# Preparation of a patch-attention kernel: one-pass prelu, weights loaded earlier, and unused matmuls in TensorE's pauses

## The reference, cut to what matters

```python
def prelu(x, a): return jnp.where(x >= 0, x, a * x)
x = gn(x)                                          # mean and variance per channel
embed_w  = prelu(conv1x1(x, Wa, ba), aa)           # 32 channels, 48 x 48
match_in = prelu(conv1x1(x, W1, b1), a1)           # 16 channels, 48 x 48
ref = prelu(conv1x1(pool2x2(x), W2, b2), a2)       # 16 channels, 24 x 24
w  = patches3x3(ref);  wn = w / max(norm(w), 1e-4) # 576 keys of 144
xp = patches3x3(match_in)                          # 2304 queries of 144
y  = softmax(10 * wn @ xp, over keys)              # 576 x 2304
# patches of embed_w, weighted by y, are overlapped and convolved with Wd (stride 2)
```

## Time and profile before

| | us |
|---|---|
| median of 3 runs (lowest, highest) | 326.76 (324.23, 326.82) |
| profiled execution | 326.36 |
| its span | 324.6 |
| PE busy | 259.4 (80%) |
| DVE busy | 173.8 (54%) |
| ACT busy | 133.1 (41%) |
| POOL busy | 98.6 (30%) |

### The profile page before, as it was taken

One profiled execution on the slowest core, in us unless ns is written; L12 is line 12 of the kernel. 1 busy time (PEld: TensorE's weight loads), 2 busy tenths in 40 slices (PEclk: granted clock), 3 DMA queues, 4 the chain that ended last, 5 costly groups with the idle time before them and its releaser, 6 DMA issues.

```text
span 324.6 us, 4740 instructions
## 1 busy us (share of the span) xinstructions
PE 259.4 (80%) x1698; PEld 240.2 (74%) x1698; DVE 173.8 (54%) x368; ACT 133.1 (41%) x269; POOL 98.6 (30%) x101
## 2 busy tenths in 40 slices
PE   0459529936396979997998999999998899998075
PEld 0448428926375859996998989999987799997074
DVE  3864623254746673377225745555696854543822
ACT  2060236254346452445335674547645442122020
POOL 2710122038546220523514051517845600000000
PEclk9999999577657575599759999999999999999655
DMA  3030034420003000134300000000120000000241
GB/s 73 0 48 3 9 67 72 104 70 2 1 0 50 2 1 0 14 61 72 56 3 0 2 0 3 0 2 0 38 37 2 0 3 0 2 0 2 44 65 36
DMA packets 11495, 7.67 MB, mean 24 GB/s; under 512 B 8497, under 2 KB 10609, under 8 KB 11345
## 3 DMA queue, kind: packets, MB, share of 16 engines
q1 hardware_dynamic: 11264, 7.09, 12.2%
q10 hardware_dynamic: 208, 0.30, 0.3%
HBM read 2.14 MB, written 1.18 MB: 10 GB/s over the span
## 4 chain that ended last, share of the span: by engine, by line
PE 51%; DVE 20%; issue 9%; SPq 9%; ACT 6%; POOL 2%; DMA 2%; DVEq 0%; ACTq 0%; POOLq 0%
PE zt L727 20%; PE yt L742 8%; PE ps L707 5%; PE pm L681 4%; SPq L377 3%; SPq L373 3%; PE pm L621 3%; DVE negm L1156 3%; PE pm L774 3%; PE pm L660 2%; DVE mimg L1078 2%; DVE yl L1171 2%; DVE bnst L988 2%; PE pd L754 2%; DVE mimg L1075 2%
## 5 line engine op out<-in xcount | busy, mean ns | idle before, releaser
L727 PE MATMUL zt<-ident,nt 128*125 128x128 f32 (+1 forms) x720 | 98.0, 290 | 0.0
L727 PEld LDWEIGHTS zt<-ident,nt 128*125 128x125 f32 (+1 forms) x720 | 94.0, 191 | 1.4 <-issue 0.3
L528 POOL TENSOR_TENSOR nt<-nt 128x599 f32<-128x599 f32 (+1 forms) x42 | 56.4, 1342 | 47.9 <-ACT nt L907 40.8
L1171 DVE TENSOR_TENSOR yl<-zt,yh 125x384 fp32r<-125x384 f32 (+1 forms) x60 | 33.4, 557 | 43.9 <-ACT yh L915 15.2
L915 ACT ACTIVATE yh<-zt 125x384 fp32r<-125x384 f32 (+1 forms) x60 | 29.2, 486 | 44.1 <-PE zt L727 44.1
L899 ACT ACTIVATE nt<-ps,negm 128x576 f32<-128x576 f32 x32 | 23.7, 742 | 56.5 <-DVE negm L1156 56.5
L707 PE MATMUL ps<-wh,mh 128*128 128x288 f32 x64 | 18.3, 372 | 17.0 <-POOL mr L522 12.3
L907 ACT ACTIVATE nt<-nt,rps 128x599 f32<-128x599 f32 x36 | 28.6, 795 | 7.1 <-DVE rps L1163 6.9
L1156 DVE TENSOR_REDUCE negm<-ps 128x1 f32<-128x576 f32 x32 | 24.1, 753 | 13.1 <-PE ps L707 13.0
L742 PE MATMUL yt<-yh,kh 125*128 125x384 f32 (+1 forms) x60 | 25.6, 427 | 4.6 <-DVE yl L1171 4.5
L1194 DVE SCALAR_TENSOR_TENSOR v<-pd,v 32x384 f32<-32x384 f32 (+3 forms) x48 | 26.3, 547 | 2.4 <-PE pd L754 0.9
...
## 6 DMA issues: line engine op xcount, KB each, us to landing
...
```

Source lines behind the costliest of these rows:

```text
L528: pool.tensor_tensor(nt[:, dst, (to + 1) * KP + 1:(to + 1) * KP + 1 + n], nt[:, one, (row1 + 1) * KP + 1:(row1 + 1) * KP + 1 + n], nt[:, o ...
L727: last = nc.tensor.matmul(turned(zt[:, m % 2, :], n, dh, col, JW), keys_at(tile, r + dr, n, shift), ident[:, :], start=at == 0, stop=at == ...
L1171: nc.vector.tensor_tensor(yl[0:n, blk, :].rearrange("p (h j) -> p h j", j=W), turned(zt[:, m % 2, :], n), F(yh[0:n, blk, :]).rearrange("p ...
```

## The change

1. **One-pass prelu.** The conv weights and biases of a convolution are multiplied by a sign (1 for slopes up to 1, else -1), so that prelu becomes the larger of `v + bias` and `slope * (v + bias)`. ACT writes `slanted = slope * v + slope * bias` (`slant`), DVE one pass, `max(v + bias, slanted)`, for each part. The signs are taken back in the keys' scale (`kscale`) and in the output weights (POOL, one product more). DVE computes the signs (`slope_signs`) before the statistics and waits there for the parameters.
2. **Match image.** The parts of `conv1` no longer write the copied rows; two DVE copies of 336 columns do, after the eighth part.
3. **Order of preparation.** `weights` is put before `low`; W2, W1, Wa are scaled and split one after another; `bias` becomes three jobs, of which the third (Wa) comes after `split`. The eight parts of `conv1` follow one another and `norm` comes behind them. In `SPREAD` the jobs of image 1 move likewise by up to two thirds of a step.
4. **Loads.** SP issues two quarters of `x`, then the output weights, all of image 1, the residual images and the cosine matrix, and only then the patches. ACT issues the other two quarters ahead of the parameters.
5. **POOL and DVE.** POOL zeroes `wdf` and the borders of `nt` at the start; `emb`, `mr`, `wr` are zeroed by DVE. POOL handles the output weights right after `mean` of image 0.
6. **Unused matmuls.** `idle(n)` issues n fp32 matmuls of 128 x 128 on `ones` into `yt`, which nothing reads: 14 before the mean, 5 before the first bias, 2 before `norm`, 6 before `inorm`, 6 and 10 before the scores.

```diff
 BEFORE = [
-    ("xs", (0,)), ("mean", (0,)), ("low", (0,)), ("weights", (0,)), ("bias", (0,)), ("conv2", (0, 1)),
-    ("conv1", (0, 1)), ("squares", (0,)), ("conv1", (2, 3, 4)), ("norm", (0,)), ("conv1", (5, 6, 7)),
-    ("inorm", (0, 1)), ("keys", (0,)), ("split", (0, 1))]
+    ("xs", (0,)), ("mean", (0,)), ("weights", (0,)), ("bias", (0, 1)), ("conv2", (0, 1)), ("low", (0,)),
+    ("conv1", (0, 1)), ("squares", (0,)), ("conv1", (2, 3, 4, 5, 6, 7)), ("norm", (0,)),
+    ("inorm", (0, 1)), ("keys", (0,)), ("split", (0, 1)), ("bias", (2,))]
+WARM = {("mean", 0): 14, ("bias", 0): 5, ("norm", 0): 2, ("inorm", 0): 6, ("keys", 0): 6, ("split", 0): 10}
...
-            load_x(0)
+            load_x(0, range(2))
+            output_weights()
+            load_x(1, range(4))
+            for b in range(B):
+                sp.dma_start(x1(b), x[b].rearrange("c h w -> c (h w)")).then_inc(s_xin[b], 16)
+            sp.dma_start(cosm[:, :], dct).then_inc(s_cos, 16)
             ref_patches(0)
             match_patches(0)
-            sp.dma_start(x1(0), x[0].rearrange("c h w -> c (h w)")).then_inc(s_xin[0], 16)
-            load_x(1)
-            output_weights()
-            sp.dma_start(cosm[:, :], dct).then_inc(s_cos, 16)
-            sp.dma_start(x1(1), x[1].rearrange("c h w -> c (h w)")).then_inc(s_xin[1], 16)
...
-            first = before.index(("low", 0, 0))
+            first = before.index(("squares", 0, 0))
+            zeros()
+            pool.wait_ge(s_tiles, NPOOL_EDGES)
             perform(before[:first], handlers)
-            zeros()
-            pool.wait_ge(s_tiles, NTILE_EDGES)
+            output_weights()
+            pool.wait_ge(s_wd, 1)
             perform(before[first:], handlers)
-            output_weights()
...
+            def idle(n):
+
+                for _ in range(n):
+                    nc.tensor.matmul(yt[:, 0:128], ones[:, :], ones[:, :], start=True, stop=True)
...
-            perform(before, handlers)
+            pe.wait_ge(s_const, 2)
+            for name, b, k in before:
+                idle(WARM.get((name, k), 0))
+                handlers.get(name, lambda b, k: None)(b, k)
             scores(0)
...
-                if k % 2:
-                    nc.scalar.activation(zneg[0:rows, 1, :], o[0:rows, 0:HALF], ACT.Relu,
-                                         bias=nbias[0:rows, which:which + 1], scale=-1.0)
-                nc.scalar.activation(z[0:rows, k % 2, :], o[0:rows, 0:HALF], ACT.Relu,
-                                     bias=bias[0:rows, which:which + 1]).then_inc(s_z, 1)
+                nc.scalar.activation(slanted[0:rows, k % 2, :], o[0:rows, 0:HALF], ACT.Identity,
+                                     bias=sbias[0:rows, which:which + 1],
+                                     scale=par[0:rows, P_A1 + which:P_A1 + which + 1]).then_inc(s_slant, 1)
...
+            for r in (2, 3):
+                src = x[0].rearrange("c h w -> c (h w)")
+                nc.scalar.dma_start(x4[0][C * r:C * (r + 1), :],
+                                    src[:, QUARTER * r:QUARTER * (r + 1)]).then_inc(s_x4[0], 16)
             nc.scalar.dma_start(par[0:96, :], params[0:96, :]).then_inc(s_par, 16)
...
+                nc.vector.scalar_tensor_tensor(out=dst, in0=o[0:rows, 0:HALF].rearrange("p (h w) -> p h w", w=w),
+                                               scalar=bias[0:rows, which:which + 1],
+                                               in1=slanted[0:rows, k % 2, :].rearrange("p (h w) -> p h w", w=w),
+                                               op0=ALU.add, op1=ALU.max).then_inc(s_free["dve"], 1)
...
                 if i == ROWS - 1:
+                    wait_emptied(dve, "conv1", b, i)
+                    n, last = CHUNK - W, CHUNK * (BLOCKS - 1)
+                    nc.vector.tensor_copy(mimg[:, 1 + W:1 + CHUNK],
+                                          mimg[:, 1 + CHUNK * NCH:1 + CHUNK * NCH + n]).then_inc(s_dup[b], 1)
+                    nc.vector.tensor_copy(mimg[:, 1 + last:1 + last + n],
+                                          mimg[:, 1 + CHUNK + W:1 + 2 * CHUNK]).then_inc(s_dup[b], 1)
```

199 lines of the change are left out of this document (102 added, 97 removed).

## The result

The changed kernel took 311.91 us in the median of 4 runs (310.07 to 314.44), the kernel before beside it 326.16 (324.23 to 326.82): ratio 0.9578, 95% interval 0.948 to 0.9676. The forecast was 312.4. The profiled execution of the changed kernel took 310.07 (span 308.3), so against the 326.36 of before it gives -16.3 where the sum had -14.0. The total is right; several terms of it are not, and they cancel. In all that follows, an execution more than 1.5% longer than the fastest of its kernel counts in the medians but not in the ratios.

A forecast was written before the change was run, and what follows sets the result against it. Bounds: image 0's preparation until first scores at 46.45, a mixed middle to about 140 us, then PE. Terms -2.4 -0.9 -4.7 -0.3 +1.2 -2.3 -2.1 -2.5 = -14.0 took 326.36 to 312.4 us; range 304 to 320.

The forecast's parts named there:

- The head: Image 0's preparation: scores 0 start at 44.0 instead of 46.45, -2.4 us.
- the first scores at 2.4 GHz: Scores 0: unused matmuls let them run at 2.4 GHz instead of 1.2, -0.9 us.
- scores 0 after 46: Start of scores 0: a start later than 46 us would show the prediction wrong.
- The price of the unused ones: Ahead of scores 0: the unused matmuls cost 0.9 us there.
- The wait for mr: PE at 67 to 73 us: early output weights remove its 5.67 us wait for POOL; scores 9 come earlier, -4.7.
- The third bias: Behind scores 9: it now stands on PE's path, with some 0.6 covered by the next exponential, +1.2 us.
- conv1, -2.3 and -2.1: Image 1's conv1: one DVE pass a part shortens PE's 2.61 wait (-2.3) and removes the other waits until 124 us (-2.1).
- no such wait would be left: Image 1's conv1: no pause of PE for DVE would show the prediction right.
- The clock in the middle: Image 1's conv1, norms and scores: without the pause PE stays at 2.4 GHz, -2.5 us, bounds 0 and -8.
- The clock stays up: Rival, conv1 through middle: fillers hold the level, norms take 3, middle gains its whole 8; 303.1 us, chance 0.12.
- The memsets: Rival, 2 to 6 us: DVE's and POOL's memsets exclude each other, signs at 8.7, +2.6; 315.0 us, chance 0.12.
- Transposes and the clock: Image 1's 18 transposes: trace disagrees that they don't count as busy; by that rule the clock term is 0, time 314.9.

The follow-up runs named there:

- no_fill: Changed kernel with all 43 unused matmuls taken out: 313.24 us, ratio 0.9605 to the kernel before.
- early_weights: Kernel before with only its output weights loaded and split early: 320.88 us, ratio 0.9784 to the kernel before.
- late_again: Changed kernel with output-weight loads and POOL's split back in the kernel before's order, second run: median 313.1 us, ratio 0.9551 to the kernel before.
- dve_load: Changed kernel with two unused DVE passes added to each part of conv1 of image 1: 318.59 us, ratio 0.9789 to the kernel before.
- mid_fill: Changed kernel with unused matmuls also in TensorE's pauses between 68 and 83 us: 307.27 to 311.98 us, ratio 0.9521 to the kernel before.
- one_fill: Changed kernel with 14 unused matmuls in the 3.54 us pause ahead of values(1,4): 311.7 us, ratio 0.9553 to the kernel before.

## Why the prediction was right, and where it was not

- **The head, -2.4, and -0.9 for the first scores at 2.4 GHz: failed.** Measured -0.4, and the second is worth nothing. The early steps were near (statistics 6.90 for 6.75, conv1 18.50 for 18.2), the match image was late already (29.76 for 28.6). Scores 0 stood at 46.07, not at 44.0; the prediction had named scores 0 after 46 as a sign of being wrong. Two steps make up the difference. The first is conv1's rounds: ScalarE's slanted copy takes 0.59, not the 0.50 of the old one, and the three rounds took 2.34, 2.66 and 2.33, not 2.18, so the norms began at 28.52, not 27.1; the 1.4 went down PE's chain unchanged (inverse norms 36.89 for 35.5, the sixteen at 39.40 for 38.0). The second is the sixteen: they took 5.76, not 5.1, since they ran at 1.2 GHz until 43.6. A third step failed beside the path: the keys' last two DVE instructions, counted as before, took 1.4 more beside POOL. The price of the unused ones, forecast 0.9, was 1.1 (no_fill).
- **The wait for mr, -4.7: right in size, wrong in cause.** Scores 6 to 9 moved by 5.3 to 5.5 more than scores 0, and the edit alone brings 5.0 at this place (early_weights). But it was put down to the early weights, and those are not needed (late_again). The prediction had the match image 10 us earlier and the loads behind it on SP in the same paragraphs, and did not put the two together: the queue was moved by its own 9.5 us.
- **The third bias, +1.2: right.** From scores 9 to 10 it was 4.13 before and is 5.38.
- **conv1, -2.3 and -2.1.** Between scores 10 and the third part 2.1 went, the first term. The second failed: PE's later waits for the match image were 2.1 in all (0.99 and 1.12) and are 1.4 (0.75 and 0.63), 0.7 less, where they were taken whole; that no such wait would be left was one of the prediction's signs, and 1.10 is left before the third part too. dve_load puts the whole of DVE's relief at 6 to 7, clock included.
- **The clock in the middle, -2.5: failed in size.** From conv1's third part to the end the trace shows -9.8; less the 2.1 counted for DVE's later waits it leaves -7.7 for the clock, less the 0.7 that went of them -9.1: at the far end of the bounds of 0 to -8, or beyond. At scores 14 all but conv1's first term was 12.5; the new pause at 132.23 and the 1.2 GHz behind it (0.52 in the window) gave 4.8 back. The direction was right, but not the reason as a rule: with the pause of 2.61 down to 1.10 the level stayed up, yet elsewhere it fell with no pause (mid_fill). Two steps were wrong. It was priced for the 8 us behind one pause, while the level in fact stayed up from 95 to 132 us, through the norms of image 1 (3.14 for 5.89), as the rival *The clock stays up* had it for this half of the kernel; image 0's norms, its other half, took 5.81. And nothing was said of what comes late when all this is early: the keys of image 1, on DVE and ScalarE, for which PE waits 3.54.
- **The memsets, weighed as a rival: out.** DVE reached the signs at 6.29, not at 8.7, and statistics at 6.90 for 6.75. Its four new memsets, 2.3 us by their own durations, are recorded as ending at 5.09, and POOL's fill 2.0 to 5.0: they ran side by side. The Trainium skill (SBUF — State Buffer, "Who interferes with whom") lets a DVE instruction with at most one SBUF input, outside the two-port modes, run beside GpSimd, and the trace agrees for memsets. The comb instruction ahead of them is recorded at 3.17 where it took 0.23 before, but it ends in the record within 0.01 of all four memsets; they can't all have run behind it, so that it was held is not shown.
- **Transposes and the clock.** The Trainium skill (TensorE: Matmul & The Clock Gate, "Part 4: PE-mode transpose") says that they don't count as busy. In the changed kernel the level rose at 95 us, inside 18 transposes, and in one_fill it did not rise there; in mid_fill it fell ahead of them. These traces don't settle it either way.

In short: the -3.3 of the head and first scores became -0.4, the clock's -2.5 and the -2.1 of conv1's later waits became -9.8 together in the profiled execution and some 2 less in a median one, and the rest stood. That the median came out 0.5 from the forecast is luck: the sum of errors of opposite sign.
